# Output projection of a decoder layer: a float32 product per tile against a product of rounded halves

## The chip, the cores and the metric

The kernel runs on one core of a Trainium2 chip. The metric is the device time of one execution in microseconds (us). Nothing is computed on the host but the layout of the inputs.

## The reference

One decoder layer with normalisation after each part, over 2 sequences of 2048 tokens with 512 features: self-attention with 16 heads, cross-attention over 154 context tokens, a mixture of 64 experts with a shared expert. The change touches only the end of the first part:

```python
out = jnp.einsum('bhqk,bkhd->bqhd', attn, v).reshape(B, T, C)
return out @ Wo.T + bo
...
x = _layernorm(x + _L0_attn_ref(x, ...), axis=-1)   # (x - mean) / sqrt(var + 1e-5)
```

Everything is float32.

## The kernel before

`program` runs one stage after another: `self_attention`, `out_proj_norm`, `cross_attention`, `route_and_shared`, `experts`, `last_norm`. Each stage has its own semaphores and one instruction stream per engine, written out by hand: an engine does its instructions in the order of the code, and a wait holds everything behind it. There is no planner.

`out_proj_norm` (from L759) works on 32 tiles of 128 tokens. Self-attention has left its result transposed in HBM (`aT`). For each tile:

- SP loads the attention rows `at` (L797, 256 KB) and the residual `xr` (L799, 256 KB), two buffers each. Behind tile 2's it issues the loads that the next stage needs: weights, biases and two masks (L803, L805), some 2.6 MB in all. Behind the last tile's it loads the next stage's first rows.
- POOL adds the output bias to the residual, a tile ahead (L828).
- PE multiplies `at` by the output weights `wo` into one of two PSUM banks (L850): four float32 matmuls of 512 columns, which run as two passes each, so eight passes a tile. It does the product of tile t + 1 before it turns (transposes) the normalised rows of tile t (L856, four blocks).
- DVE adds product and residual (L876), takes mean and variance (L878, L881), inverts the deviation that ACT's square root gives (L895, L883) and normalises (L887).
- ACT stores the normalised rows (L897), copies the turned rows out of PSUM (L900) and stores them too (L902).

Ahead of the tiles, PE makes the cross-attention keys (L842) and DVE takes them out of PSUM (L870). `each_tile` writes tiles 0 to 2 and 29 to 31 out in straight code and runs the others in a rolled loop, two tiles a pass, in which waits compare with a register. `cross_attention` already does its own output projection as a product of halves (L1096, L1198, L1296) and its normalisation with Ln, Exp and a scaled copy on ACT (L1264, L1266, L1272).

Of the kernel before, what the change touches and what calls it, by code (L numbers as in the profile page):

```python
# [12 lines left out]
P = 128  # L13
# [689 lines left out]
        body(t, t % 2)  # L703


def before_end(t, ahead=0):
    return not isinstance(t, int) or t + ahead < NT

# [48 lines left out]


def out_proj_norm(nc, sems, early, cross, aT, x, bo, x1, x1T, mask, wqT, woT, bq, bk, bv, bo2):  # L759
    with ExitStack() as ctx:  # L760
        def sb(name, shape, dt=F32):
            return ctx.enter_context(nc.sbuf_tensor("on_" + name, shape, dt))
# [2 lines left out]
        passed = sem("passed")  # L765
        wo = early.o_weights; bob = sb("bob", [P, DM])
        identf, eps = cross.identf, cross.eps
        at = sb("at", [P, 2, KT, P]); xr = sb("xr", [P, 2, DM]); xb = sb("xb", [P, 2, DM])
        y = sb("y", [P, 2, DM]); stats = sb("stats", [P, 2, 6]); mv = sb("mv", [P, 2, 2])
        rstd = sb("rstd", [P, 2]); std = sb("std", [P, 2])  # L770
        xn = sb("xn", [P, 2, DM]); xnT = sb("xnT", [P, 2, KT, P])
        ops = [ctx.enter_context(nc.psum_tensor(f"on_o{i}", [P, DM], F32)) for i in range(2)]
        tps = [ctx.enter_context(nc.psum_tensor(f"on_t{i}", [P, DM], F32)) for i in range(2)]
        kps = [ctx.enter_context(nc.psum_tensor(f"on_k{i}", [P, 512], F32)) for i in range(NG)]
        w_in = sem("w_in"); k_done = sem("k_done"); ident_set = sem("ident_set"); a_in = [sem(f"a_in{i}") for i in range(2)]
        x_in = [sem(f"x_in{i}") for i in range(2)]
        o_done = sem("o_done"); xb_done = sem("xb_done"); y_done = sem("y_done"); nstep = sem("nstep"); mv_done = sem("mv_done"); std_done = sem("std_done"); rstd_done = sem("rstd_done")
        xn_done = sem("xn_done"); t_done = sem("t_done"); xnT_done = sem("xnT_done")
        xn_out = [sem(f"xn_out{i}") for i in range(2)]; xnT_out = [sem(f"xnT_out{i}") for i in range(2)]
        block = ctx.enter_context(nc.Block())  # L780
# [10 lines left out]
        @block.sync  # L791
        def _(sp):
            sp.dma_start(cross.bkb[:], bk).then_inc(w_in, 16)
            sp.dma_start(bob[:], bo.partition_broadcast(P)).then_inc(w_in, 16)
            def body(t, s):
                wait(sp, o_done, t - 1)
                sp.dma_start(at[:, s], aT.rearrange("k p t -> p k t")[:, :, bass.ds(t * P, P)]).then_inc(a_in[s], 16)  # L797
                wait(sp, xb_done, t - 1)
                sp.dma_start(xr[:, s], x[bass.ds(t * P, P), :]).then_inc(x_in[s], 16)  # L799
                if isinstance(t, int) and t == LEAD - 1:  # L800
                    for dst, src in ((cross.bvb[:], bv.partition_broadcast(P)), (cross.bqb[:], bq), (cross.wq[:], wqT),
                                     (cross.wo[:], woT), (cross.bob[:], bo2.partition_broadcast(P))):
                        sp.dma_start(dst, src).then_inc(cross.w_in, 16)  # L803
                    for n in range(2):
                        sp.dma_start(cross.mk[:, n], mask[n * P:(n + 1) * P, :]).then_inc(cross.mk_in[n], 16)  # L805
                if isinstance(t, int) and t == NT - 1:
                    for n in range(2):
                        sp.wait_ge(xnT_out[n], 16)
                        apart(sp, passed)
                        sp.dma_start(cross.xT[:, n], x1T[n]).then_inc(cross.xT_in[n], 16)  # L810
                        sp.wait_ge(xn_out[n], 16)
                        apart(sp, passed)
                        sp.dma_start(cross.xr[:, n], x1[n * P:(n + 1) * P, :]).then_inc(cross.x_in[n], 16)
            each_tile(sp, body)

        @block.gpsimd
        def _(pool):
# [19 lines left out]
        @block.tensor  # L837
        def _(pe):
            pe.wait_ge(early.first_in, 64)
            for g in range(NG):  # L840
                for k in range(KT):
                    mm = nc.tensor.matmul(kps[g][:, 0:BATCH * CTX], early.k_weights[:, k, g * P:(g + 1) * P],  # L842
                                          early.ctx[:, k].rearrange("p b c -> p (b c)"), start=k == 0, stop=k == KT - 1)
                mm.then_inc(k_done, 1)
            pe.wait_ge(ident_set, 3)
            def product(t, s):
                fetched(pe, a_in, t, s)
                wait(pe, y_done, t - 1)
                for k in range(KT):
                    mm = nc.tensor.matmul(ops[s][:], at[:, s, k], wo[:, k], start=k == 0, stop=k == KT - 1)  # L850
                mm.then_inc(o_done, 1)
            def turn(t, s):
                pe.wait_ge(xn_done, t + 1)
                wait(pe, xnT_done, t - 1)
                for k in range(KT):
                    mm = nc.tensor.transpose(tps[s][:, k * P:(k + 1) * P], xn[:, s, k * P:(k + 1) * P], identf[:])  # L856
                mm.then_inc(t_done, 1)
            product(0, 0)
            def body(t, s):
                if before_end(t, 1):  # L860
                    product(t + 1, 1 - s)
                turn(t, s)
            each_tile(pe, body)

        @block.vector
        def _(dve):
            dve.wait_ge(w_in, 32)
            for g in range(NG):
                dve.wait_ge(k_done, g + 1)
                dve.tensor_scalar(cross.keys[:, g].rearrange("p b c -> p (b c)"), kps[g][:, 0:BATCH * CTX],  # L870
                                  cross.bkb[:, g:g + 1], float(HD) ** -0.5, ALU.add, ALU.mult).then_inc(cross.set_up, 1)

            def body(t, s):
                dve.wait_ge(o_done, t + 1)
                dve.wait_ge(xb_done, t + 1)
                dve.tensor_tensor(y[:, s], ops[s][:], xb[:, s], ALU.add).then_inc(y_done, 1)  # L876
                dve.wait_ge(y_done, t + 1)
                dve.bn_stats(stats[:, s], y[:, s]).then_inc(nstep, 1)  # L878
                dve.wait_ge(nstep, t + 1)
                apart(dve, passed)  # L880
                dve.bn_aggr(mv[:, s], stats[:, s]).then_inc(mv_done, 1)  # L881
                dve.wait_ge(std_done, t + 1)
                dve.reciprocal(rstd[:, s:s + 1], std[:, s:s + 1]).then_inc(rstd_done, 1)  # L883
                dve.wait_ge(rstd_done, t + 1)
                stored(dve, xn_out, t, s)
                wait(dve, t_done, t - 1)
                dve.tensor_scalar(xn[:, s], y[:, s], mv[:, s, 0:1], rstd[:, s:s + 1], ALU.subtract, ALU.mult).then_inc(xn_done, 1)  # L887
            each_tile(dve, body)

        @block.scalar  # L890
        def _(act):
            act.wait_ge(ident_set, 3)
            def body(t, s):
                act.wait_ge(mv_done, t + 1)
                nc.scalar.activation(std[:, s:s + 1], mv[:, s, 1:2], ACT.Sqrt, bias=eps[:]).then_inc(std_done, 1)  # L895
                act.wait_ge(xn_done, t + 1)
                act.dma_start(x1[bass.ds(t * P, P), :], xn[:, s]).then_inc(xn_out[s], 16)  # L897
                act.wait_ge(t_done, t + 1)
                stored(act, xnT_out, t, s)
                nc.scalar.copy(xnT[:, s].rearrange("p k t -> p (k t)"), tps[s][:]).then_inc(xnT_done, 1)  # L900
                act.wait_ge(xnT_done, t + 1)
                act.dma_start(x1T[t], xnT[:, s]).then_inc(xnT_out[s], 16)  # L902
            each_tile(act, body)
            for s in range(2):
                act.wait_ge(xn_out[s], 16 * (NT // 2))
                act.wait_ge(xnT_out[s], 16 * (NT // 2))
# [1235 lines left out]
```

## Time and profile before

| | us |
|---|---|
| median of 3 runs | 3286.88 |
| lowest, highest | 3275.59, 3287.71 |
| the profiled execution | 3281.05 |
| its span, first to last instruction | 3279.3 |
| busy: PE, DVE, ACT, POOL | 2963.8, 2039.8, 1453.1, 1520.5 |
| mean granted TensorE clock | 0.961 of full speed |

The span is the profiler's own, from the first instruction to the last; the device time also holds what lies around it. Busy times are sums over the whole span, in which `out_proj_norm` is the stretch from about 1708 to 1862 us. The columns of each view are named at its first group of rows.

### The profile page before, as it was taken

Reading aid. Unit: us, or ns where it says so; the run is one execution under the profiler, and the core shown is the slowest. Engines: PE = TensorE matmul, PEld = TensorE weight load, DVE = VectorE, ACT = ScalarE, POOL = GpSimd, SP = SyncE. Lnnn points to the kernel's source line nnn. Section 1 sums busy time; section 2 is a strip of 40 time slices with the busy share of each in tenths; the row PEclk is TensorE's granted clock in tenths of the full one; section 3 lists DMA queues with packets and bytes.
Section 4 is the critical chain, followed back from the end, with each engine's and each line's share of the span. In section 5 each row is a group of like instructions: output and inputs, shape, how many; then the busy total and the mean of one; then the engine's idle time right before and its main releaser. Section 6 shows DMA issues by size and latency. Waiting matters only on the chain. (4 is left out here: it accounts for less than half of the span.)

```text
span 3279.3 us, 59175 instructions
## 1 busy us (share of the span) xinstructions
PE 2963.8 (90%) x19197; PEld 1934.0 (59%) x19197; DVE 2039.8 (62%) x4795; ACT 1453.1 (44%) x3375; POOL 1520.5 (46%) x1093
## 2 busy tenths in 40 slices
PE   7998999989989999898988979999799994999992
PEld 4444444444444444444434468888688883888882
DVE  4645646556465574554725568888477774777776
ACT  1443544434444444444442257777322222555551
POOL 3343443424434344243452234444377774665656
PEclk8999999999999999999999989999999996999996
DMA  4223022221221212212207522222222224999997
GB/s 114 62 64 82 7 74 79 58 63 32 75 78 44 66 44 74 78 31 67 66 30 253 189 84 88 79 82 84 84 71 68 68 61 140 258 254 259 257 254 265
DMA packets 185030, 343.33 MB, mean 105 GB/s; under 512 B 36136, under 2 KB 54696, under 8 KB 183848
## 3 DMA queue, kind: packets, MB, share of 16 engines
q1 hardware_dynamic: 135336, 250.90, 25.7%
q0 software_dynamic: 28800, 48.43, 6.8%
q10 hardware_dynamic: 20736, 41.95, 3.3%
q8 instruction: 92, 1.51, 0.2%
q14 instruction: 66, 0.54, 0.1%
HBM read 206.96 MB, written 83.89 MB: 89 GB/s over the span
## 5 line engine op out<-in xcount | busy, mean ns | idle before, releaser
L548 ACT ACTIVATE sa_probs<-sa_s 128x512 f32<-128x512 f32 (+3 forms) x1280 | 609.8, 540 | 692.9 <-PE sa_s L440 353.1
L334 POOL TENSOR_TENSOR sa_both<-sa_probs 128x2048 f32<-128x2048 f32 (+2 forms) x160 | 590.0, 3687 | 628.4 <-ACT sa_probs L548 616.9
L406 PE MATMUL sa_w<-sa_parts 96*128 96x512 f32 (+3 forms) x1280 | 515.0, 440 | 81.7 <-DVE sa_pmax L607 43.2
L440 PE MATMUL sa_s<-sa_parts 128*128 128x512 f32 (+3 forms) x1280 | 480.4, 409 | 27.3 <-ACT sa_probs L548 21.4
L607 DVE CUSTOM_DVE_ANT_0 sa_w<-sa_w,sa_maskS 128x512 f32<-128x512 f32 (+3 forms) x512 | 327.5, 649 | 238.7 <-PE sa_w L406 234.2
L406 PEld LDWEIGHTS sa_w<-sa_parts 96*128 96x128 f32 x1280 | 232.3, 195 | 409.4 <-issue 202.5
L611 DVE TENSOR_REDUCE sa_pmax<-sa_w 128x1 f32<-128x512 f32 (+3 forms) x768 | 422.7, 585 | 47.1 <-PE sa_w L406 44.0
L440 PEld LDWEIGHTS sa_s<-sa_parts 128*128 128x128 f32 x1280 | 242.0, 193 | 168.1 <-ACT sa_probs L548 96.6
L1519 POOL DMA_INDIRECT token_and_weight_of_slot<-rt_entry,rt_sl x256 | 261.0, 1020 | 124.4 <-issue 91.3
L458 PE MATMUL sa_pv<-sa_probs,sa_values 128*32 128x512 f32 (+3 forms) x2560 | 284.2, 538 | 0.0
L1252 ACT ACTIVATE xa_sm<-xa_sm,xa_nmax 128x154 f32<-128x154 f32 x512 | 209.4, 414 | 54.9 <-DVE xa_nmax L1175 54.9
L1831 POOL DMA_INDIRECT scratch_residual<-ex_y,ex_target x90 | 162.1, 1801 | 140.8 <-DMA scratch_residual<-ex_y,ex_target 109.2
L331 POOL COPY sa_both<-sa_probs 128x512 f32<-128x512 f32 x64 | 39.1, 611 | 342.7 <-ACT sa_probs L548 333.3
L1011 POOL TENSOR_TENSOR xa_pmain<-xa_sm,xa_rrec 128x2048 f32<-128x2048 f32 x32 | 115.9, 3622 | 109.8 <-DVE xa_rrec L1179 109.8
L469 PE MATMUL sa_pv<-sa_both,sa_ones 128*32 128x512 f32 (+1 forms) x1280 | 155.0, 556 | 0.0
L1893 PE MATMUL ex_yps<-ex_w2h,ex_hTh 128*128 128x512 f32 x540 | 148.1, 412 | 4.6 <-ACT ex_hTh L1926 4.3
L1876 PE MATMUL ex_h<-ex_xeT,ex_w1h 128*128 128x256 f32 x1080 | 145.4, 284 | 2.4 <-ACT ex_w1h L1905 2.4
L1041 PE MATMUL xa_qps<-cross_xT,cross_wq 128*128 128x128 f32 x1024 | 128.9, 281 | 20.4 <-DMA cross_xT<-scratch_x_T 16.2
L1876 PE MATMUL ex_h<-ex_xeT,ex_w3h 128*128 128x256 f32 x1080 | 145.3, 283 | 0.0
L1876 PEld LDWEIGHTS ex_h<-ex_xeT,ex_w1h 128*128 128x128 f32 x1080 | 139.7, 190 | 6.7 <-issue 2.8
L1876 PEld LDWEIGHTS ex_h<-ex_xeT,ex_w3h 128*128 128x128 f32 x1080 | 136.8, 190 | 0.0
L1041 PEld LDWEIGHTS xa_qps<-cross_xT,cross_wq 128*128 128x128 f32 x1024 | 123.1, 197 | 21.3 <-issue 21.3
(236 smaller groups left out, 5360.0 us busy)
## 6 DMA issues: line engine op xcount, KB each, us to landing
list_w<-in_w SPq DMA_DIRECT2D x138, 512.0 KB, 5.6
sa_parts<-early_halves SPq DMA_DIRECT2D x384, 128.0 KB, 2.4
early_xt<-in_xT SPq DMA_DIRECT2D x32, 1024.0 KB, 5.7
scratch_attention_T<-sa_oT SPq DMA_DIRECT2D x32, 256.0 KB, 2.4
on_at<-scratch_attention_T SPq DMA_DIRECT2D x32, 256.0 KB, 3.1
on_xr<-in_x SPq DMA_DIRECT2D x32, 256.0 KB, 3.4
scratch_x<-on_xn ACTq DMA_DIRECT2D x32, 256.0 KB, 2.1
scratch_x_T<-on_xnT ACTq DMA_DIRECT2D x32, 256.0 KB, 3.4
```

The costliest lines, as they stand in the source:

```text
L334: pool.tensor_tensor(both[:, p % 2, :, 0:w], probs[:, even, :, 0:w], probs[:, odd, :, 0:w], ALU.add).then_inc(both_ready, 1)
L406: nc.tensor.matmul(ps[:, 0:w], qparts[0:3 * HD, h, q0:q0 + P], kparts[0:3 * HD, h, k0:k0 + w], start=True, stop=True).then_inc(work_ready, 1)
L440: mm = nc.tensor.matmul(ps[:, 0:w], kparts[:, h, kb * P:(kb + 1) * P], qparts[:, h, q0:q0 + w], start=True, stop=not diag)
L458: mm = nc.tensor.matmul(pvbank[0][a:a + HD, 0:w], values[:, kb, h, :], probs[:, r % NPB, h, 0:w], start=kb == NKB - 1, stop=kb == QB * chu ...
L548: nc.scalar.activation(probs[:, r % NPB, h, 0:w], sbank[n % NSB][:, 0:w], ACT.Exp).then_inc(exp_done, 1)
L607: dve.tensor_tensor_reduce(out=wbank[b][:, 0:width_], in0=wbank[b][:, 0:width_], in1=maskS[:, 0:width_], scale=1.0, scalar=LOWEST, op0=ALU ...
L611: dve.tensor_reduce(pmax[:, j * GH + h, s:s + 1], wbank[b][:, 0:width_], AX.X, ALU.max).then_inc(work_free[b], 1)
L1041: mm = nc.tensor.matmul(qps[:, g * P:(g + 1) * P], wq[:, k, g * P:(g + 1) * P], xT[:, s, k], start=k == 0, stop=k == KT - 1)
L1252: nc.scalar.activation(sm[:, s, h], sm[:, s, h], ACT.Exp, bias=nmax[:, s, h:h + 1], accum_out=rsum[:, s, h:h + 1]).then_inc(exp_done, 1)
L1519: pool.indirect_dma_start(out=table, out_offset=bass.IndirectOffsetOnAxis(ap=sl[:, s, k:k + 1], axis=0), in_=entry[:, s, k], in_offset=Non ...
L1831: pool.indirect_dma_start(out=res, out_offset=bass.IndirectOffsetOnAxis(ap=target[:, s, j:j + 1], axis=0), in_=y[:, s, j], in_offset=None, ...
L1876: mm = nc.tensor.matmul(bank[f][:, 0:UNIT], wt[:, s, a, k, f * P:(f + 1) * P], xeT[:, s, b, k], start=k == 0 and n == 0, stop=k == KT - 1 ...
```

## The change

Only `out_proj_norm` changes, with a new loop helper. The attention rows and the weights are each split into a rounded part (float32r, index 0, made by ACT) and what is left of it (index 1, the difference made by DVE). The product becomes the sum of three terms, high by high, high by low and low by high: twelve matmul passes instead of eight. The rows are loaded two tiles ahead into four buffers; the halves have two. PE runs the product two tiles ahead of the turn. ACT computes the inverse deviation as Exp(-0.5 Ln(var + eps)) and normalises by a scaled copy; DVE makes the shift that this copy needs. Each engine's order within a tile is new, and the rolled loop takes four tiles a pass: tiles 0 to 3 and 28 to 31 are straight code.

```diff
+def each_tile_of_four(eng, body):
+    for t in range(4):
+        body(t, t)
+    with eng.Fori(0, (NT - 8) // 4) as i:
+        for s in range(4):
+            body(eng.snap(i * 4 + (4 + s)), s)
+    for t in range(NT - 4, NT):
+        body(t, t % 4)
...
+    TERMS = ((0, 0), (0, 1), (1, 0))
...
-        at = sb("at", [P, 2, KT, P]); xr = sb("xr", [P, 2, DM]); xb = sb("xb", [P, 2, DM])
+        at = sb("at", [P, 4, KT, P]); ath = sb("ath", [P, 2, 2, KT, P], F32R); woh = sb("woh", [P, 2, KT, DM], F32R); xr = sb("xr", [P, 2, DM]); xb = sb("xb", [P, 2, DM])
...
-        rstd = sb("rstd", [P, 2]); std = sb("std", [P, 2])
+        rstd = sb("rstd", [P, 2]); logv = sb("logv", [P, 2]); shift = sb("shift", [P, 2])
...
-        w_in = sem("w_in"); k_done = sem("k_done"); ident_set = sem("ident_set"); a_in = [sem(f"a_in{i}") for i in range(2)]
+        w_in = sem("w_in"); k_done = sem("k_done"); ident_set = sem("ident_set"); a_in = [sem(f"a_in{i}") for i in range(4)]
...
         def _(sp):
             sp.dma_start(cross.bkb[:], bk).then_inc(w_in, 16)
             sp.dma_start(bob[:], bo.partition_broadcast(P)).then_inc(w_in, 16)
-            def body(t, s):
-                wait(sp, o_done, t - 1)
-                sp.dma_start(at[:, s], aT.rearrange("k p t -> p k t")[:, :, bass.ds(t * P, P)]).then_inc(a_in[s], 16)
+            def load_attention(t, s4):
+                wait(sp, a_low, t - 3)
+                sp.dma_start(at[:, s4], aT.rearrange("k p t -> p k t")[:, :, bass.ds(t * P, P)]).then_inc(a_in[s4], 16)
+            for t in range(2):
+                load_attention(t, t)
+            def body(t, s4):
+                s = s4 % 2
+                if before_end(t, 2):
+                    load_attention(t + 2, (s4 + 2) % 4)
                 wait(sp, xb_done, t - 1)
                 sp.dma_start(xr[:, s], x[bass.ds(t * P, P), :]).then_inc(x_in[s], 16)
                 if isinstance(t, int) and t == LEAD - 1:
...
                         sp.wait_ge(xn_out[n], 16)
                         apart(sp, passed)
                         sp.dma_start(cross.xr[:, n], x1[n * P:(n + 1) * P, :]).then_inc(cross.x_in[n], 16)
-            each_tile(sp, body)
+            each_tile_of_four(sp, body)
         @block.gpsimd
         def _(pool):
...
                                           early.ctx[:, k].rearrange("p b c -> p (b c)"), start=k == 0, stop=k == KT - 1)
                 mm.then_inc(k_done, 1)
             pe.wait_ge(ident_set, 3)
-            def product(t, s):
-                fetched(pe, a_in, t, s)
+            def product(t, s4):
+                s = s4 % 2
+                pe.wait_ge(a_high, t + 1)
+                pe.wait_ge(a_low, t + 1)
                 wait(pe, y_done, t - 1)
-                for k in range(KT):
-                    mm = nc.tensor.matmul(ops[s][:], at[:, s, k], wo[:, k], start=k == 0, stop=k == KT - 1)
+                for n, (a, b) in enumerate(TERMS):
+                    for k in range(KT):
+                        mm = nc.tensor.matmul(ops[s][:], ath[:, s, a, k], woh[:, b, k], start=k == 0 and n == 0,
+                                              stop=k == KT - 1 and n == len(TERMS) - 1)
                 mm.then_inc(o_done, 1)
             def turn(t, s):
                 pe.wait_ge(xn_done, t + 1)
...
                 for k in range(KT):
                     mm = nc.tensor.transpose(tps[s][:, k * P:(k + 1) * P], xn[:, s, k * P:(k + 1) * P], identf[:])
                 mm.then_inc(t_done, 1)
+            pe.wait_ge(wo_high, 1)
+            pe.wait_ge(wo_low, 1)
             product(0, 0)
-            def body(t, s):
-                if before_end(t, 1):
-                    product(t + 1, 1 - s)
-                turn(t, s)
-            each_tile(pe, body)
+            product(1, 1)
+            def body(t, s4):
+                if before_end(t, 2):
+                    product(t + 2, (s4 + 2) % 4)
+                turn(t, s4 % 2)
+            each_tile_of_four(pe, body)
         @block.vector
         def _(dve):
+            dve.wait_ge(wo_high, 1)
+            dve.tensor_tensor(woh[:, 1], wo[:], woh[:, 0], ALU.subtract).then_inc(wo_low, 1)
             dve.wait_ge(w_in, 32)
             for g in range(NG):
                 dve.wait_ge(k_done, g + 1)
                 dve.tensor_scalar(cross.keys[:, g].rearrange("p b c -> p (b c)"), kps[g][:, 0:BATCH * CTX],
                                   cross.bkb[:, g:g + 1], float(HD) ** -0.5, ALU.add, ALU.mult).then_inc(cross.set_up, 1)
-            def body(t, s):
+            def measure(t, s):
                 dve.wait_ge(o_done, t + 1)
                 dve.wait_ge(xb_done, t + 1)
+                wait(dve, xn_done, t - 1)
                 dve.tensor_tensor(y[:, s], ops[s][:], xb[:, s], ALU.add).then_inc(y_done, 1)
                 dve.wait_ge(y_done, t + 1)
                 dve.bn_stats(stats[:, s], y[:, s]).then_inc(nstep, 1)
                 dve.wait_ge(nstep, t + 1)
                 apart(dve, passed)
                 dve.bn_aggr(mv[:, s], stats[:, s]).then_inc(mv_done, 1)
-                dve.wait_ge(std_done, t + 1)
-                dve.reciprocal(rstd[:, s:s + 1], std[:, s:s + 1]).then_inc(rstd_done, 1)
+            def shifts(t, s):
                 dve.wait_ge(rstd_done, t + 1)
-                stored(dve, xn_out, t, s)
-                wait(dve, t_done, t - 1)
-                dve.tensor_scalar(xn[:, s], y[:, s], mv[:, s, 0:1], rstd[:, s:s + 1], ALU.subtract, ALU.mult).then_inc(xn_done, 1)
-            each_tile(dve, body)
+                dve.wait_ge(mv_done, t + 1)
+                dve.tensor_scalar(shift[:, s:s + 1], mv[:, s, 0:1], rstd[:, s:s + 1], -1.0, ALU.mult, ALU.mult).then_inc(shift_done, 1)
+            def low_half(t, s4):
+                dve.wait_ge(a_high, t + 1)
+                dve.tensor_tensor(ath[:, s4 % 2, 1], at[:, s4], ath[:, s4 % 2, 0], ALU.subtract).then_inc(a_low, 1)
+            for t in range(2):
+                low_half(t, t)
+            def body(t, s4):
+                s = s4 % 2
+                if before_end(t, 2):
+                    low_half(t + 2, (s4 + 2) % 4)
+                measure(t, s)
+                if not isinstance(t, int) or t > 0:
+                    shifts(t - 1, 1 - s)
+            each_tile_of_four(dve, body)
+            shifts(NT - 1, (NT - 1) % 2)
         @block.scalar
         def _(act):
             act.wait_ge(ident_set, 3)
-            def body(t, s):
+            def deviation(t, s):
                 act.wait_ge(mv_done, t + 1)
-                nc.scalar.activation(std[:, s:s + 1], mv[:, s, 1:2], ACT.Sqrt, bias=eps[:]).then_inc(std_done, 1)
+                nc.scalar.activation(logv[:, s:s + 1], mv[:, s, 1:2], ACT.Ln, bias=eps[:]).then_inc(log_done, 1)
+                act.wait_ge(log_done, t + 1)
+                wait(act, shift_done, t - 1)
+                nc.scalar.activation(rstd[:, s:s + 1], logv[:, s:s + 1], ACT.Exp, scale=-0.5).then_inc(rstd_done, 1)
+            def norm(t, s):
+                act.wait_ge(shift_done, t + 1)
+                stored(act, xn_out, t, s)
+                wait(act, t_done, t - 1)
+                nc.scalar.activation(xn[:, s], y[:, s], ACT.Identity, bias=shift[:, s:s + 1], scale=rstd[:, s:s + 1]).then_inc(xn_done, 1)
                 act.wait_ge(xn_done, t + 1)
                 act.dma_start(x1[bass.ds(t * P, P), :], xn[:, s]).then_inc(xn_out[s], 16)
+            def store_turned(t, s):
                 act.wait_ge(t_done, t + 1)
                 stored(act, xnT_out, t, s)
                 nc.scalar.copy(xnT[:, s].rearrange("p k t -> p (k t)"), tps[s][:]).then_inc(xnT_done, 1)
                 act.wait_ge(xnT_done, t + 1)
                 act.dma_start(x1T[t], xnT[:, s]).then_inc(xnT_out[s], 16)
-            each_tile(act, body)
+            nc.scalar.preload_act_table_set("natural_log_exp_and_others")
+            act.wait_ge(early.first_in, 64)
+            nc.scalar.copy(woh[:, 0], wo[:]).then_inc(wo_high, 1)
+            def high_half(t, s4):
+                act.wait_ge(a_in[s4], ((t - s4) // 4) * 16 + 16)
+                wait(act, o_done, t - 1)
+                nc.scalar.copy(ath[:, s4 % 2, 0], at[:, s4]).then_inc(a_high, 1)
+            for t in range(2):
+                high_half(t, t)
+            def body(t, s4):
+                s = s4 % 2
+                if before_end(t, 2):
+                    high_half(t + 2, (s4 + 2) % 4)
+                deviation(t, s)
+                if not isinstance(t, int) or t > 0:
+                    norm(t - 1, 1 - s)
+                    store_turned(t - 1, 1 - s)
+            each_tile_of_four(act, body)
+            norm(NT - 1, (NT - 1) % 2)
+            store_turned(NT - 1, (NT - 1) % 2)
             for s in range(2):
                 act.wait_ge(xn_out[s], 16 * (NT // 2))
                 act.wait_ge(xnT_out[s], 16 * (NT // 2))
```

## Rows read from the trace of the kernel before

**Rows 1.** Windows, steady part of the stage: length, busy by engine, granted clock, DMA, GB/s

```profile
1770.00:1790.00 20.00, 20.00 (x63) 9.84 (x62) 11.99 (x27) 4.96 (x11) 6.92 (x6) 1.00 0.79 269
```

**Rows 2.** Waits in the stage: engine line <- releaser: total us, times, longest

```profile
DVE on_y L876 <- PE on_o L850: 34.4, 31, 9.3
```

**Rows 3.** Timeline, two steady tiles: start, length (us), engine, line, operation

```profile
1784.92 0.69 DVE L876 TENSOR_TENSOR on_y<-on_o,on_xb 128x512 f32<-128x512 f32 x1 [0.78 <-PE on_o L850]
...
1786.90 0.29 ACT L895 ACTIVATE on_std<-on_mv,cross_eps 128x1 f32<-128x1 f32 x1 [0.85 <-DVE on_mv L881]
...
1788.59 0.60 PE L856 MATMUL on_t<-cross_identf,on_xn 128*128 128x128 f32 x4
1788.80 0.69 DVE L876 TENSOR_TENSOR on_y<-on_o,on_xb 128x512 f32<-128x512 f32 x1 [0.59 <-PE on_o L850]
...
1789.03 3.60 PE L850 MATMUL on_o<-early_xt,on_at 128*128 128x512 f32 x8
...
1789.35 0.59 ACT L900 COPY on_xnT<-on_t 128x512 f32<-128x512 f32 x1 [2.16 <-PE on_t L856]
...
1790.10 0.34 ACTq L902 DMA_DIRECT2D scratch_x_T<-on_xnT  x1
...
1790.59 0.29 ACT L895 ACTIVATE on_std<-on_mv,cross_eps 128x1 f32<-128x1 f32 x1 [0.65 <-DVE on_mv L881]
...
1791.35 0.55 DVE L887 TENSOR_SCALAR on_xn<-on_y,on_mv,on_rstd 128x512 f32<-128x512 f32 x1 [0.27 <-DVE on_rstd L883]
...
1792.04 0.14 PEld L856 LDWEIGHTS on_t<-cross_identf,on_xn 128*128 128x128 f32 x1 [0.24 <-DVE on_xn L887]
```

**Rows 4.** Timeline, the product that starts after the stall

```profile
1739.08 6.37 PE L850 MATMUL on_o<-early_xt,on_at 128*128 128x512 f32 x8 [6.51 <-DMA on_at<-scratch_attention_T]
```

**Rows 5.** Windows, the stall: the columns of rows 1

```profile
1732.00:1736.00 4.00, 0.57 (x5) 0.34 (x3) 2.08 (x5) 0.88 (x2) 0.00 (x0) 1.00 1.02 401
1736.00:1740.00 4.00, 0.92 (x1) 0.50 (x2) 0.20 (x1) 0.00 (x0) 0.19 (x1) 0.71 1.09 378
```

**Rows 6.** Timeline, the start of the stage

```profile
1718.99 0.45 PEld L850 LDWEIGHTS on_o<-early_xt,on_at 128*128 128x128 f32 x2
...
1719.45 0.54 DVE L870 TENSOR_SCALAR cross_keys<-on_k,cross_bkb 128x308 f32<-128x308 f32 x1 [1.54 <-PE on_k L842]
```

**Rows 7.** Timeline, the last tile of the stage

```profile
1857.80 0.66 PE L856 MATMUL on_t<-cross_identf,on_xn 128*128 128x128 f32 x4 [2.52 <-DVE on_xn L887]
1858.49 0.59 ACT L900 COPY on_xnT<-on_t 128x512 f32<-128x512 f32 x1 [1.53 <-PE on_t L856]
1859.11 0.34 ACTq L902 DMA_DIRECT2D scratch_x_T<-on_xnT  x1
```

**Rows 8.** Timeline, cross attention: its product of halves and its normalisation

```profile
2058.70 0.29 ACT L1264 ACTIVATE xa_logv<-xa_mv,cross_eps 128x1 f32<-128x1 f32 x1
...
2058.87 3.01 PE L1096 MATMUL xa_ops<-xa_woh,xa_oTh 128*128 128x512 f32 x12
2059.02 0.20 ACT L1266 ACTIVATE xa_rstd<-xa_logv 128x1 f32<-128x1 f32 x1
...
2059.68 0.82 ACT L1272 ACTIVATE xa_xn<-xa_y,xa_shift,xa_rstd 128x512 f32<-128x512 f32 x1 [0.45 <-DVE xa_shift L1194]
...
2060.68 0.34 ACTq L1276 DMA_DIRECT2D scratch_x<-xa_xn  x1
2061.11 0.59 ACT L1296 CAST xa_oTh<-xa_pvps 128x512 fp32r<-128x512 f32 x1 [0.62 <-ACT xa_xn L1272]
```

**Rows 9.** Groups by shape, casts and differences: count, busy, mean ns, idle before

```profile
L1905 ACT CAST ex_w3h<-list_w 128x1024 fp32r<-128x1024 f32 x46 | 48.1, 1045 | 0.0
...
L1926 ACT CAST ex_hTh<-ex_hT 128x256 fp32r<-128x256 f32 x90 | 36.3, 403 | 38.1 <-DVE ex_hT L1975 38.1
```

**Rows 10.** Timeline, the split of the weights in cross attention

```profile
1863.78 1.90 ACT L1304 CAST xa_woh<-cross_wo 128x2048 fp32r<-128x2048 f32 x1
1865.78 2.29 DVE L1234 TENSOR_TENSOR xa_woh<-cross_wo,xa_woh 128x2048 fp32r<-128x2048 f32 x1 [8.04 <-ACT xa_woh L1304]
```

More of the change, by code:

```diff
@@ L774, in out_proj_norm @@
         kps = [ctx.enter_context(nc.psum_tensor(f"on_k{i}", [P, 512], F32)) for i in range(NG)]
-        w_in = sem("w_in"); k_done = sem("k_done"); ident_set = sem("ident_set"); a_in = [sem(f"a_in{i}") for i in range(2)]
+        w_in = sem("w_in"); k_done = sem("k_done"); ident_set = sem("ident_set"); a_in = [sem(f"a_in{i}") for i in range(4)]
         x_in = [sem(f"x_in{i}") for i in range(2)]
-        o_done = sem("o_done"); xb_done = sem("xb_done"); y_done = sem("y_done"); nstep = sem("nstep"); mv_done = sem("mv_done"); std_done = sem("std_done"); rstd_done = sem("rstd_done")
+        o_done = sem("o_done"); xb_done = sem("xb_done"); y_done = sem("y_done"); nstep = sem("nstep"); mv_done = sem("mv_done"); a_high = sem("a_high"); a_low = sem("a_low"); wo_high = sem("wo_high"); wo_low = sem("wo_low"); log_done = sem("log_done"); rstd_done = sem("rstd_done"); shift_done = sem("shift_done")
         xn_done = sem("xn_done"); t_done = sem("t_done"); xnT_done = sem("xnT_done")
```

## The prediction

> **What bounds the kernel now.** I read the page first, then the windows, the waits and the timeline of the stage that the change touches. The page's own chain of waits only reaches back over the last normalisation of the kernel, so it says nothing here. The windows show the stage's steady part to be TensorE's: busy 20.00 us of 20 at a granted clock of 1.00, DVE 12 us, ACT 5 us, DMA share 0.79 [rows 1]. The waits agree: the longest in the stage that is not some idle engine's own is DVE's for the product, 34.4 us [rows 2]. The timeline gives the period: the add of L876 starts at 1784.92 and again at 1788.80, 3.88 us a tile, of which eight passes of the product are 3.60 us [rows 3]. One stretch is not TensorE's. The cross-attention weights are loaded behind tile 2's rows, DMA is full, and the product that should have started at about 1732.6 starts at 1739.08 after 6.51 us of waiting [rows 4]; while it waits, the granted clock stays 1.00 in one window and falls to a mean of 0.71 in the next [rows 5], so that the product takes 6.37 instead of 3.60 us. The stall costs about 6.5 + 2.8 = 9.3 us. The first product starts at 1718.99 [rows 6], the last store is issued at 1859.11 [rows 7].
>
> **The change, part by part.** *Product.* Twelve passes on rounded halves replace eight. The trace has such a product in cross attention: twelve in 3.01 us [rows 8], against 3.60 [rows 3]. TensorE gains 0.6 us a tile; with the turn (0.60, or about 0.43 where the next pass overlaps it) its own work is about 3.4 us.
>
> *What the halves cost.* ACT gets a cast of 512 columns a tile: between 403 ns (256) and 1045 (1024) [rows 9], by a straight line 0.62 us. DVE gets a difference of 512, as wide as the add of 0.69 us [rows 3]. DVE loses the normalising operation (0.55) [rows 3] and the reciprocal; ACT gets it at 0.82 us, and Ln with Exp, 0.52 us from the start of one to the end of the other [rows 8], for Sqrt (0.29).
>
> *Order.* This is what decides, so I wrote each engine's new order down. Within one tile step ACT does: cast(t+2), Ln and Exp(t), normalise(t-1), copy and store of the turned rows (t-1). DVE: difference(t+2), add, statistics and aggregate(t), shift(t-1). PE: product(t+2), turn(t). An engine takes its instructions in order, so a wait at the head holds all behind it. Follow one ring: turn(t-2) frees ACT's copy(t-2); behind it on ACT stands cast(t+2); DVE's difference(t+2) waits for that cast, and behind the difference on DVE stands the add of tile t, though its product is long done; Ln(t) waits for the aggregate(t); behind Ln and Exp(t) on ACT stands normalise(t-1); turn(t-1) waits for that. From turn(t-2) to turn(t-1) is one tile, and nothing on the way overlaps anything else on the way. The second buffers do not open the ring, because it closes by order and not by a buffer. Product(t+1) runs beside it, between the two turns.
>
> The length of the ring has two versions, for the tiles in straight code (the hops as in rows 7) and those in the rolled loop (as in rows 3). Turn's start to the copy: 0.69 [rows 7], 0.76 [rows 3]. Copy's start to its store's issue: 0.62, 0.75. Issue 0.34 and 0.09 until ACT's next instruction (2060.68 + 0.34 to 2061.11) [rows 8]: 0.43. Cast 0.62. Hop to DVE: 0.03 (1858.46 to 1858.49), 0.14 (end of the normalising operation 1791.90 to 1792.04). Difference 0.69 and 0.03 of gap. Add to the deviation's start: 1.79 for one tile, 1.98 for the other [rows 3], taken as 1.79 and as the mean, 1.88. Ln and Exp 0.52. Normalise 0.05 + 0.82. Hop to PE 0.03, 0.14. Sums: 6.33 and 6.83 us; with 1.98 it is 6.93. The ring is thus nearly twice TensorE's present 3.88, and the gain of the product is idle time.
>
> *The start.* The weights' cast (1.90) and difference (2.29) [rows 10] lie beside the key products, which end at about 1719.4; the cover has several us to spare. But DVE takes the differences of tiles 0 and 1 only behind its fourth key operation, which ends at 1719.45 + 0.54 = 1719.99 [rows 6]. So product(0) starts at about 1720.8 instead of 1719.0, ends at 1723.8; cast(2) 0.62 and difference(2) 0.69 with a hop, then add(0) at 1725.2, Ln(0) at 1727.1, Exp ends at 1727.6; cast(3) and difference(3) to 1729.0, Ln(1) at 1730.9, Exp ends 1731.4, normalise(0), turn(0) at 1732.3.
>
> *The sum.* Turns 1 to 3 are straight code: 3 x 6.33 = 19.0. Tiles 4 to 27 are rolled: 24 x 6.83 = 163.9. Turn 28: 6.3. From tile 30 there is no cast ahead: add(30) waits only for normalise(28), and turns 29 and 30 follow at 0.05 + 1.88 + 0.52 + 0.87 and a hop, 3.4 us each; turn 31 after copy, issue and normalise, 2.7 us. So turn(31) starts at 1931.0, and its store is issued 1.31 later [rows 7]: 1932.3, against 1859.11. That is 73 us longer. All tiles at 6.33 make it 61 us, all at 6.93 make it 76.
>
> *Loads.* Tiles 0 to 4 are now fetched before the cross-attention weights. SP waits for a difference two tiles back, long done. The rows of tile 5 and the residual of tile 3 are issued behind the weights at about 1727; in the present run everything issued there had landed by 1740 [rows 5], and tile 3's add is due only at about 1742. So the stall of 9.3 us goes, but into the ring, which is late next; the 73 us are counted from ends and contain it already. POOL's add is done a tile ahead. A megabyte a tile at 6.8 us asks for half the DMA share of now. The store's two issues on ACT: the one of the turned rows is in the ring, the other lies beside the turn. The table load of the present Sqrt goes, and may go once more at the start of cross attention; neither stands on a path that ends a stage.
>
> The profiled run took 3281.05 us (span 3279.3), 5.8 below the median of the runs, 3286.88. 3281 + 73 = 3354.
>
> **Rivals.** *A, the ring with a slow clock.* TensorE would work some 3.4 us and then rest some 3.4 us in each tile. In the stall the clock was still 1.00 in the first window of the rest and fell in the second [rows 5]; a shorter rest that comes back in every tile is in no row of mine. At the lower level a product took 6.37 for 3.60 [rows 4], a factor of 1.77. Twelve passes would take 5.3 and the turn 1.2 us, still under the ring; only the turn's 0.5 us lies in the ring, 28 x 0.5 = 14 us more: 3368. For it: the rest comes in every tile. Against: at the lower level TensorE would work 6.5 of 7.3 us, which is not what stood before the fall in rows 5.
> The Trainium skill (page TensorE: Matmul & The Clock Gate, section "HAM oscillation — how this bites in real kernels") says that a loop in which the array has to wait in every pass is put back to the slow clock in every pass. By that rule rival A holds and the time is 3368; by the row alone, with the clock held, it is 3354.
>
> *B, on the other side: the steps overlap after all.* If the ring spanned two tiles (a wait that I place at the head of a queue being met earlier than I think), the bound would be the fullest engine. That is ACT: cast 0.62, Ln and Exp 0.52, normalise 0.87, copy 0.59, two issues at 0.43 and up to 0.3 of hops, 3.4 to 3.8 us, against 3.88 now. Over 28 tiles that gives 2 to 13 us, and the stall's 9.3 less 2 at the start: 3281 - 17 = 3264. It decides from the point at which the ring falls under 3.9 us. For it: every engine's own work is below that, and no engine but ACT comes near. Against: each link of the ring is written as a wait or as an order.
>
> *C, half of it:* a link or two, such as the store's issue, don't stand in series: 5.3 to 6.2 us a tile, by the same sum 3313 to 3339. *D, the product doesn't gain:* if the twelve took 3.6 or more, the time would not change, as TensorE rests; it would show in the product's row alone.
>
> **How the numbers follow.** Forecast 0.73 (own range 3341 to 3364), A 0.13, C 0.07, B 0.07. About 0.5%, 16 us, is what a measurement of this kernel can tell from no change. Only B is below that bound: faster 0.06, same 0.02, slower 0.92. The range from 3332 to 3376 holds the forecast, most of A and the upper end of C.
>
> **What would show it.** Right: in the windows of the stage TensorE busy about half, all engines with idle time, and about 6.8 us from add to add; the waits headed by the turn for the normalised rows, by the difference for the cast, and by the copy for the turn; the add of tile t starting right behind difference(t+2), with its product done one tile before; the DMA share near 0.45 and no stall at 1732; turns of the last three tiles at 3.4 and 2.7 us. Wrong: a period below 5.5 us, or an add that starts when its product ends, would mean that the ring is not closed; a period above 7.2 with a clock near 0.5 would mean A.

## The result, and the profile after

| | us |
|---|---|
| median after (4 runs) | 3345.45 (3343.63 to 3348.20) |
| median before, same chip (4 runs) | 3284.93 (3275.59 to 3287.71) |
| ratio after to before | 1.0191, 95% interval 1.0169 to 1.0212 |
| profiled execution after | 3346.18, span 3344.4, mean clock 0.953 |

The change makes the kernel 60 us slower. Between the two profiled executions it is 65.1 us, in the span as in the whole time, and nearly all of it lies in the one stage: from the first product to the issue of the last store are now 206.9 us (1719.07 to 1926.00), against 140.1 [rows 6, 7].

Three windows of the stage after, with the columns of [rows 1]:

```profile
1730.00:1750.00 20.00, 12.18 (x51) 9.36 (x52) 7.00 (x15) 7.33 (x15) 5.36 (x4) 0.90 0.78 248
...
1770.00:1790.00 20.00, 12.21 (x50) 8.97 (x49) 6.99 (x15) 7.58 (x16) 3.81 (x3) 0.91 0.49 161
...
1810.00:1830.00 20.00, 12.91 (x47) 9.73 (x46) 6.99 (x15) 6.84 (x16) 3.80 (x3) 0.78 0.48 158
```

PE was busy 20.00 of 20 us; now, over the nine windows from 1730 to 1910, it is busy 11.38 to 14.29 us, and DVE, ACT and POOL less than half. In the steady windows DMA moves some 160 GB/s where it moved 269. A stage in which nothing is full is waiting for itself, and the waits from 1719 to 1920 say where (the columns of [rows 2]):

```profile
POOL on_xb L849 <- DVE on_y L907: 145.5, 27, 7.4
DVE on_ath L921 <- ACT on_ath L968: 118.4, 30, 4.4
ACT on_logv L941 <- DVE on_mv L912: 73.4, 31, 2.4
PE on_t L881 <- ACT on_xn L950: 67.8, 29, 3.6
...
ACT on_xnT L957 <- PE on_t L881: 27.6, 30, 1.3
...
DVE on_y L907 <- PE on_o L874: 1.5, 1, 1.5
```

Read from the bottom: DVE's wait for the product, 34.4 us before [rows 2], is gone. The four lines above it hand on to each other: the difference waits for the cast, the logarithm for the statistics, the turn for the normalised rows, the copy for the turn. POOL, at the head, waits for the add, and nothing waits for POOL: no line of the view names it behind the arrow. The timeline of one tile, from turn to turn, shows them in their order:

```profile
1776.96 4.48 PE L874 MATMUL on_o<-on_woh,on_ath 128*128 128x512 f32 x12
...
1782.68 0.65 PE L881 MATMUL on_t<-cross_identf,on_xn 128*128 128x128 f32 x4 [1.24 <-ACT on_xn L950]
...
1783.09 3.03 PE L874 MATMUL on_o<-on_woh,on_ath 128*128 128x512 f32 x12
1783.37 0.59 ACT L957 COPY on_xnT<-on_t 128x512 f32<-128x512 f32 x1 [0.82 <-PE on_t L881]
1784.11 0.34 ACTq L959 DMA_DIRECT2D scratch_x_T<-on_xnT  x1
1784.69 0.62 ACT L968 CAST on_ath<-on_at 128x512 fp32r<-128x512 f32 x1 [0.74 <-ACT on_xnT L957]
1785.34 0.69 DVE L921 TENSOR_TENSOR on_ath<-on_at,on_ath 128x512 fp32r<-128x512 f32 x1 [4.01 <-ACT on_ath L968]
1785.95 0.68 DVE L907 TENSOR_TENSOR on_y<-on_o,on_xb 128x512 f32<-128x512 f32 x1
...
1787.74 0.29 ACT L941 ACTIVATE on_logv<-on_mv,cross_eps 128x1 f32<-128x1 f32 x1 [2.43 <-DVE on_mv L912]
1788.06 0.20 ACT L944 ACTIVATE on_rstd<-on_logv 128x1 f32<-128x1 f32 x1
...
1788.17 0.80 ACT L950 ACTIVATE on_xn<-on_y,on_shift,on_rstd 128x512 f32<-128x512 f32 x1
...
1789.10 0.65 PE L881 MATMUL on_t<-cross_identf,on_xn 128*128 128x128 f32 x4 [2.99 <-ACT on_xn L950]
1789.51 4.60 PE L874 MATMUL on_o<-on_woh,on_ath 128*128 128x512 f32 x12
```

From the first turn on, every line but the products follows on the one above it, with at most 0.24 us between them (the statistics between add and logarithm are left out here). The product (3.03 us, 3.60 before in [rows 3]) lies beside them. The add of L907 has no wait of its own: it starts as the difference ends. Its product is the first line, which was over at 1781.44, 4.5 us earlier. That product and the one in the last line, 4.48 and 4.60 us, ran in part at the lower clock: from 1789.50 to 1794.20 the granted clock is 0.64.

The stage's two ends:

```profile
1719.07 8.44 PE L874 MATMUL on_o<-on_woh,on_ath 128*128 128x512 f32 x36 [1.32 <-DVE on_ath L921]
...
1729.95 0.66 PE L881 MATMUL on_t<-cross_identf,on_xn 128*128 128x128 f32 x4 [2.44 <-ACT on_xn L950]
...
1924.23 1.12 PE L881 MATMUL on_t<-cross_identf,on_xn 128*128 128x128 f32 x4 [1.98 <-ACT on_xn L950]
...
1926.00 0.34 ACTq L959 DMA_DIRECT2D scratch_x_T<-on_xnT  x1
```

The stall of [rows 4] is gone, as three products' worth of rows stand ready; nobody can tell from the time, since the ring was later anyway.

### The profile page after: what moved, and what is told of

Read it like the earlier page. It is cut to its first block and busy times, and to the rows that moved or that the text cites. A ratio compares the mean times of both kernels' runs of the same rounds, so it can differ in the third digit from the quotient of the medians.

```text
span 3344.4 us, 59553 instructions
## 1 busy us (share of the span) xinstructions
PE 2972.4 (89%) x19325; PEld 1975.1 (59%) x19325; DVE 2042.4 (61%) x4796; ACT 1505.8 (45%) x3472; POOL 1520.3 (45%) x1093
```

## The experiments

"Stage" is the time from the first product to the start of the last copy of turned rows: 139 to 140 us before, 206 after. The kernel before, timed beside them, had medians of 3280.0 to 3282.6; after was not timed again beside them, so that differences from its 3345.45 carry some 2 to 5 us of scatter, and the stage, read from the traces, is the closer measure.

| run | median, us | ratio to before, 95% | stage, us |
|---|---|---|---|
| after | 3345.45 | 1.0191, 1.0169 to 1.0212 | 206.3 |
| e1_add_first | 3276.71 | 0.9993, 0.9982 to 1.0004 | 133.9 |
| e4_issue_late | 3320.28 | 1.0132, 1.0115 to 1.0148 | 180.1 |
| e2_product_twice | 3350.88 | 1.0224, 1.0206 to 1.0241 | 210.4 |
| e3_one_term | 3353.40 | 1.0234, 1.0217 to 1.0251 | 213.9 |
| e5_order | 3303.66 | 1.0060, 1.0045 to 1.0076 | 165.7 |
| e7_both | 3264.21 | 0.9942, 0.9926 to 0.9957 | 123.6 |
| e9_no_ring_weights | 3291.39 | 1.0031, 1.0019 to 1.0042 | 149.8 |
| e6_loads_ahead | 3281.45, one run | | 135.8 |
| e10_both_weights_later | 3257.55 | 0.9926, 0.9913 to 0.9938 | 116.8 |
| e11_before_weights_later | 3283.17 | 1.0005, 0.9994 to 1.0015 | 142.8 |

**The ring opened on DVE.** Only the order of DVE's instructions changes:

```diff
-                if before_end(t, 2):
-                    low_half(t + 2, (s4 + 2) % 4)
                 measure(t, s)
                 if not isinstance(t, int) or t > 0:
                     shifts(t - 1, 1 - s)
+                if before_end(t, 2):
+                    low_half(t + 2, (s4 + 2) % 4)
```

> DVE does the add, the statistics and the shift of a tile ahead of the difference two tiles on; nothing else is changed. Ring by order: the difference, the add and the statistics leave the ring, and what is left from turn to turn is copy, issue, cast, Ln, Exp and normalise, about 0.7 + 0.75 + 0.43 + 0.62 + 0.05 + 0.5 + 0.05 + 0.8 + 0.14 = 4.1 us a tile for 6.6 now: 3345 - 28 x 2.5 = 3275 (3268 to 3285), and the add starts while ACT copies. Added work (each engine simply has more to do in a tile, whatever the order): every instruction is still there, 3345. Slow clock: TensorE rests less, but its clock alone was worth 0.5 us in every second tile: not below 3335.

It took 3276.71 us: all of the loss is gone, with the same instructions on every engine, and the stage is 72.4 us shorter than in after. The timeline of this run, from turn to turn:

```profile
1782.21 0.65 PE L881 MATMUL on_t<-cross_identf,on_xn 128*128 128x128 f32 x4 [0.18 <-ACT on_xn L950]
1782.21 0.69 DVE L907 TENSOR_TENSOR on_y<-on_o,on_xb 128x512 f32<-128x512 f32 x1 [0.63 <-ACT on_xn L950]
...
1784.22 0.62 ACT L968 CAST on_ath<-on_at 128x512 fp32r<-128x512 f32 x1 [0.74 <-ACT on_xnT L957]
1784.75 0.29 ACT L941 ACTIVATE on_logv<-on_mv,cross_eps 128x1 f32<-128x1 f32 x1
...
1786.11 0.65 PE L881 MATMUL on_t<-cross_identf,on_xn 128*128 128x128 f32 x4 [0.51 <-ACT on_xn L950]
```

The add now starts with the turn, not 3.3 us behind it, and the statistics are ready when ACT has done its cast, so that the logarithm waits for nothing. The period is 3.90 us; what is left of the ring is turn, copy, issue, cast, Ln, Exp and normalise.

**The ring shortened on ACT.** The store of the turned rows is issued one step later, behind the next cast:

```diff
...
                 if before_end(t, 2):
                     high_half(t + 2, (s4 + 2) % 4)
+                if not isinstance(t, int) or t > 1:
+                    issue_turned(t - 2, s)
                 deviation(t, s)
...
```

> ACT issues the store of the turned rows behind the next cast in place of ahead of it, in the time in which it waits for the statistics; nothing else is changed. Ring by order: only the wait for the copy and the issue leave the ring, 0.43 to 0.73 us from the copy's end to the cast's start less about 0.1, so 0.3 to 0.6 a tile: 3345 - 28 x 0.5 = 3331 (3326 to 3338). Added work or a slow clock: ACT is busy 7.5 us of 20, its issue lies in idle time either way, 3345.

It took 3320.28, 25 us less than after (26.2 in the stage), and about 11 less than expected. Copy, cast and issue in this run:

```profile
1781.90 0.59 ACT L957 COPY on_xnT<-on_t 128x512 f32<-128x512 f32 x1 [0.82 <-PE on_t L881]
1782.38 0.62 ACT L970 CAST on_ath<-on_at 128x512 fp32r<-128x512 f32 x1
1782.65 0.34 ACTq L961 DMA_DIRECT2D scratch_x_T<-on_xnT  x1
```

In after the cast started 0.73 us behind the end of the copy; here it starts 0.11 before it. An issue between these two ACT instructions costs not its 0.34 us but 0.84 here: the wait for the copy's result, the issue, the start of the next, and the overlap that copy and cast have in a row. Over the 28 such gaps the mean is 0.71 us in after and -0.10 in this run, 0.80 a tile and 22.5 us in all, most of what was measured. The prediction's link had the wait and the issue, but not that overlap.

**Is the product on the path?** Two kernels change the arithmetic's size alone, to 24 passes and to 4:

```diff
-    TERMS = ((0, 0), (0, 1), (1, 0))
+    TERMS = ((0, 0), (0, 1), (1, 0)) * 2
```

> The three terms of the product are summed twice, 24 passes a tile (the projected rows are doubled, nothing else is changed). Ring by order: 24 passes are some 5.6 us between two turns and still end before the next turn is due, so nothing gets longer; TensorE hardly rests, its clock holds, all turns take 0.66 in place of 1.1 in every second tile, and the period falls from a mean of 6.6 to 6.4: 3345 - 7 = 3338 (3332 to 3346), granted clock of the stage 1.0. Product on the path (the twelve passes are part of what a tile takes): 32 x 2.6 = 83 us more, 3428.

```diff
-    TERMS = ((0, 0), (0, 1), (1, 0))
+    TERMS = ((0, 0),)
```

> Only the high by high term of the product is left, 4 passes a tile (the two low terms are left out; both halves are still made). Ring by order: no gain from a third of the product; TensorE rests longer, more turns run at the lower clock, the period goes to 6.6 to 6.9: 3345 to 3354. Product on the path: 32 x 8 x 0.216 = 55 us less, 3290.

Twice the product adds 5 us, a third of it takes nothing off: away from the stage's ends it is not on the path. Twice the product missed its expectation in sign. One window of each (columns of [rows 1]), 24 passes first, then 4:

```profile
1790.00:1810.00 20.00, 18.71 (x86) 14.54 (x85) 6.99 (x15) 7.75 (x16) 3.88 (x3) 1.00 0.49 160
```

```profile
1790.00:1810.00 20.00, 8.46 (x24) 5.73 (x24) 6.12 (x15) 7.41 (x15) 3.62 (x3) 0.51 0.48 157
```

With 24 passes PE is nearly always busy, the clock stays at 1.00 (2.4 GHz), every turn but the last takes 0.60 to 0.66 us, and turns 1 to 28 take 180.9 us against after's 185.1: a gain of 4.2 where I expected 7. So the slow clock is not what makes after slow, either. What I left out are the ends, where PE's queue is the path: turn(0) stands behind three products of 5.5 us and comes 16.5 us after the first product instead of 10.9; the turn of tile 29 comes 6.0 after its forerunner instead of 3.2; and the stage started 2 us later. -4.2 + 5.6 + 2.8 + 2.1 is 6.3, of which the profiled executions show 5.3. With 4 passes the granted clock is 0.51 in this window (0.50 to 0.74 in those from 1730 to 1850), every turn takes 1.11 or 1.12 us, as after's turns at the lower level (1.2 GHz) do, and the mean period is 6.9.

**A better order that is none.** On top of the first experiment, ACT does Ln and Exp, the normalise, then the cast, and the copy last:

```diff
-                if before_end(t, 2):
-                    high_half(t + 2, (s4 + 2) % 4)
                 deviation(t, s)
                 if not isinstance(t, int) or t > 0:
                     norm(t - 1, 1 - s)
+                if before_end(t, 2):
+                    high_half(t + 2, (s4 + 2) % 4)
+                if not isinstance(t, int) or t > 0:
                     store_turned(t - 1, 1 - s)
```

> As the run with the add ahead of the difference, and ACT also makes the cast of the tile two on behind the normalise of the tile before, so that the cast leaves the ring and lies beside the turn. Ring by order: ACT's own chain is left, Ln and Exp 0.5, normalise and its issue 1.3, cast 0.6, copy and its issue 1.3, about 3.7 us a tile for 3.9: 3277 - 28 x 0.2 = 3271 (3262 to 3278). The loads of the cross-attention weights hold the residual of tile 3 as before. If what is left after the first cut is not ACT's order but TensorE or DMA: 3277.

It took 3303.66, 33 more than expected: a miss. The waits from 1770 to 1830 name it:

```profile
DVE on_ath L921 <- ACT on_ath L968: 30.8, 12, 2.8
ACT on_logv L941 <- DVE on_mv L912: 23.5, 12, 2.0
```

As in after, only POOL's wait for the add stands ahead of these two in the list. With the cast behind the normalise there is a second ring: add(t), statistics, Ln and Exp(t), normalise(t-1), cast(t+2), difference(t+2) on DVE, and behind that on DVE the add(t+1). One tile again, 5.3 us (turns at 1782.41 and 1787.74). I had moved an instruction out of one ring and had not drawn the other. The same mistake stands in the next kernel, which has four buffers for `y` so that an add need not wait for an earlier normalise, issues the turned rows' store between Ln and Exp, and loads the next stage's two weights later. Its core:

```diff
...
+                deviation(t, s, s4)
+                if not isinstance(t, int) or t > 0:
+                    norm(t - 1, 1 - s, (s4 + 3) % 4)
                 if before_end(t, 2):
                     high_half(t + 2, (s4 + 2) % 4)
-                deviation(t, s)
                 if not isinstance(t, int) or t > 0:
-                    norm(t - 1, 1 - s)
-                    store_turned(t - 1, 1 - s)
+                    store(t - 1, 1 - s)
+                    copy_turned(t - 1, 1 - s)
...
```

> An attempt at a faster version: the add ahead of the difference, four buffers for the sum of product and residual, ACT's order Ln, issue of the turned rows two back, Exp, normalise, cast, issue, copy; and the two large cross-attention weights are loaded behind tile 3 and tile 28 and not both behind tile 2. Ring by order: no ring shorter than TensorE's own work is left, 3.1 to 3.3 us a tile, DMA share about 0.95, and tile 3's residual no longer waits (5 us): 3277 - 28 x 0.65 - 5 = 3254 (3246 to 3262). If DMA cannot give a megabyte in 3.3 us beside the work, 3.5 to 3.9 us a tile: 3262 to 3272.

It took 3291.39, 37 more than expected. The same two links, from add to add:

```profile
1783.71 0.68 DVE L910 TENSOR_TENSOR on_y<-on_o,on_xb 128x512 f32<-128x512 f32 x1
...
1787.01 0.60 ACT L977 CAST on_ath<-on_at 128x512 fp32r<-128x512 f32 x1
...
1787.64 0.69 DVE L924 TENSOR_TENSOR on_ath<-on_at,on_ath 128x512 fp32r<-128x512 f32 x1 [2.04 <-ACT on_ath L977]
...
1788.25 0.68 DVE L910 TENSOR_TENSOR on_y<-on_o,on_xb 128x512 f32<-128x512 f32 x1
```

4.5 us, and no buffer in it: the fourth `y` could not help.

**Both edits together**, the first experiment's and the late issue:

> The two cuts tried one by one, together: the add ahead of the difference, and the turned rows' store issued behind the next cast. Ring by order: the period falls from 3.9 us by the 0.8 that the late issue was worth alone, until DVE's add waiting for the normalise two tiles back and TensorE's own 3.1 to 3.4 us hold it: 3.3 to 3.4 us, 3277 - 28 x 0.5 = 3263 (3256 to 3270). If the two cuts were worth the same thing (the second hides what the first removed): 3277.

It took 3264.21, within 1.2 us. Turns come every 3.35 us (1781.32, 1784.67, 1788.04), and the window reads

```profile
1770.00:1790.00 20.00, 19.93 (x96) 15.05 (x95) 17.88 (x31) 14.10 (x30) 7.93 (x7) 1.00 0.96 314
```

PE is full again, now at 3.4 us a tile instead of 3.88: with the ring cut in both places the gain of the product shows. One stall is left, at tile 3, where the residual's rows stand behind the next stage's weights:

```profile
1738.88 0.69 DVE L907 TENSOR_TENSOR on_y<-on_o,on_xb 128x512 f32<-128x512 f32 x1 [7.92 <-POOL on_xb L849]
```

**That stall.** Two kernels ask for it on the side of before. The first gives before the attention rows two tiles ahead, in four buffers, with the loop of four tiles that they need, and nothing else:

```diff
...
+                if before_end(t, 2):
+                    load_attention(t + 2, (s4 + 2) % 4)
...
```

> The kernel before with one part of the change alone: attention rows loaded two tiles ahead into four buffers. The product of tile 3 no longer waits at 1732 to 1739, but its add still needs the residual that is loaded behind the weights and lands at about 1740: the stage's stall shrinks from 9 to about 5 us, the period stays 3.87, 3277 by one look. If the rows alone made the stall, it goes wholly, 3272.

The product of tile 3 no longer waits, but its add does: the same line reads 1742.52 with 4.95 us for POOL, whose residual is late. The stage is 3.4 us shorter; one run can't resolve that. The second leaves before's loads in place and issues `wo` of the next stage behind tile 29 instead of tile 2:

```diff
...
+                if isinstance(t, int) and t in (LEAD - 1, NT - 3):
+                    dst, src = (cross.wq[:], wqT) if t == LEAD - 1 else (cross.wo[:], woT)
+                    sp.dma_start(dst, src).then_inc(cross.w_in, 16)
```

> The kernel before with only this: the second large cross-attention weight is loaded behind tile 29 and not behind tile 2. It shows what the loads alone are worth: half of the bytes ahead of tile 3's rows, so the stall of 9.3 us falls to some 4: 3282 - 5 = 3277 (3272 to 3281). If the stall has another cause than these bytes: 3282.

No gain, 1.0005: a miss. The products behind the two loads:

```profile
1739.80 3.70 PE L853 MATMUL on_o<-early_xt,on_at 128*128 128x512 f32 x8 [3.64 <-DMA on_at<-scratch_attention_T]
...
1851.67 6.55 PE L853 MATMUL on_o<-early_xt,on_at 128*128 128x512 f32 x8 [4.88 <-DMA on_at<-scratch_attention_T]
```

The first stall is 3.64 instead of 6.51 [rows 4] and keeps its clock; the second is new. With rows one tile ahead each load in the line stalls by itself.

**The best of it.** Both edits, with `wq` issued behind tile 3 and `wo` behind tile 28:

> The two cuts together, and the two large cross-attention weights loaded behind tile 3 and behind tile 28 and not both behind tile 2. With the two cuts the add of tile 3 waited 7.9 us for a residual behind these loads, and the clock fell after it. Ring by order, stall now open: the wait goes or falls to 1 to 2 us, 3264 - 8 = 3256 (3251 to 3261). If the wait only moves to the tile behind the one weight that is left there: 3264.

3257.55 us, 0.74% less than before and 88 less than after. The stretch of the stall is now

```profile
1730.00:1750.00 20.00, 18.76 (x92) 14.40 (x91) 14.39 (x29) 13.16 (x29) 7.89 (x6) 1.00 0.99 340
```

with PE at work and the clock held, as the rows stand two tiles ahead.

## Why the prediction was right, step by step

The time was 3345.45, in the forecast's own range of 3341 to 3364 and 8.6 below its 3354.

*The ring.* It is there, link by link, in the order that the prediction wrote down. Its two cuts are what shows it: without one instruction more or less, the order on DVE alone makes the stage 72 us shorter, the issue's place on ACT alone 26. Rival B (steps that overlap) and the bound by an engine fall with that, and with 4 and 24 passes, which move the time by 5 to 8 us, not by the 55 less or 83 more of a product on the path. C falls too: the mean period of 6.61 us lies above its 6.2, and the issue that it took out of the series stands in it.

*Its length* was the term that was off. Predicted 6.83 us a rolled tile; four turns at the full clock in a row (1789.10 to 1815.15) take 6.29, 6.95, 6.39 and 6.42, in the mean 6.51. The links of the tile from 1782.68:

| link | predicted | measured |
|---|---|---|
| turn to copy | 0.76 | 0.69 |
| copy to issue | 0.75 | 0.74 |
| issue to cast | 0.43 | 0.58 |
| cast to difference | 0.76 | 0.65 |
| difference to add | 0.72 | 0.61 |
| add to Ln | 1.88 | 1.79 |
| Ln to normalise | 0.57 | 0.43 |
| normalise to turn | 0.96 | 0.93 |
| sum | 6.83 | 6.42 |

I took a gap between instructions in a row on one engine where two of them overlap by 0.08 us, and the mean of two values for add to deviation where the lower holds. Against that, every fourth tile is longer by some 0.6 (6.95 of the four above): where the rolled loop comes round, ACT's cast starts 0.56 us behind the end of the issue instead of 0.09 to 0.24 (1784.11 + 0.34 to 1784.69), and the rest lies in the gaps around Exp and the normalise. I did not have that link; that the loop's own turn-round makes it is argued from its place, not shown by a run.

*The sum.* The last store was to be issued at 1932.3 and was at 1926.00. Of the 6.3 us, 2.35 are the start: the first product at 1719.07 instead of 1720.8, and 10.9 instead of 11.5 us from there to turn(0). The first of these lies within scatter: the first products of the kernels here start anywhere from 1719.1 to 1723.0. 4.1 are turns 1 to 28, 185.1 us instead of 189.2: the rolled ones were shorter by 4.4 in all, the straight ones longer by 0.3. The last three turns came in 9.15 instead of 9.5, with 3.23, 3.28 and 2.64 us for the predicted 3.4, 3.4 and 2.7; and the last turn was slow by 0.46. The stages behind gave back another 1.8 us, and the four runs' medians, not the profiled ones, differ by 60.5 instead of 65.1. In the sum itself the straight links add up to 6.32, not 6.33, and the 76 us given for all tiles at 6.93 hold for the rolled ones alone (all 28 make it 78).

*Luck.* Two terms that the sum did not hold made up for part of what its links had too much: the slow turns, 4.1 us, and the loop's come-round, about 6 x 0.55 = 3.3 us. By this estimate the median would else have been near 3338, below the forecast's own range. The mechanism does not hang on that; the fit of the number does.

*Rival A* was true in part. Turns of 1.11 or 1.12 us appear, eight of the 28, with two in between (0.85, 0.98): 8 x 0.45 + 0.2 + 0.3 = 4.1 us of the 14 that it priced. The clock fell and came back from tile to tile, with a window's mean of 0.78 to 0.91. The Trainium skill (page TensorE: Matmul & The Clock Gate, section "HAM oscillation — how this bites in real kernels") tells its rule, by which the clock falls again in every pass, of a loop whose wait is long enough, a condition that the prediction left out. The turns of the kernel with 4 passes, all slow, agree with it; those of this one, eight slow of 28, do not.

*Product, start, loads, D:* twelve passes took 3.03 us (3.01 predicted). The split of the weights stayed hidden: its difference was over at 1712.81, and the 1.32 us of wait ahead of the first product are for the first tile's difference. The stall went into the ring. That the loads had landed by 1740 is not to be read from [rows 5], which hold no landing; in the trace before, POOL's wait for the residual ended at 1739.81. POOL's longest wait for the residual is 12.1 us and no add waits for it. The gain of the product was worth nothing as long as the ring was whole.

*What would show it:* PE is busy 57 to 71% rather than half, since its passes at the lower clock count longer; the DMA share is 0.45 to 0.50 from 1750 on, as predicted. The mean period is 6.61, not 6.8.

## What to carry to other kernels

When a change spreads a tile's work over more engines, write each engine's order down and follow, from any instruction, what it waits for or stands behind, until you come back to it one tile on: the longest such way is the period, however idle the engines, unless one engine's own work in a tile is longer still. A further buffer that is no link of that way does not help, as the fourth `y` did not here. Then do the same for the order that you want to put in its place: two of the orders here cut one ring and closed another. And an operation that is cheap by its duration (a DMA issue on ACT) is to be priced by the link that it adds between its neighbours, 0.8 us for 0.34.

## What the runs showed of the hardware

*DVE beside POOL.* In the kernel with both edits the difference, 0.69 us in after, takes 0.68 to 1.81. It is long where POOL's bias add runs at the time:

```profile
1782.66 1.29 POOL L849 TENSOR_TENSOR on_xb<-on_xr,on_bob 128x512 f32<-128x512 f32 x1 [1.61 <-DMA on_xr<-in_x]
...
1783.31 1.18 DVE L921 TENSOR_TENSOR on_ath<-on_at,on_ath 128x512 fp32r<-128x512 f32 x1
...
1786.40 1.30 POOL L849 TENSOR_TENSOR on_xb<-on_xr,on_bob 128x512 f32<-128x512 f32 x1 [2.45 <-DMA on_xr<-in_x]
...
1786.82 1.42 DVE L921 TENSOR_TENSOR on_ath<-on_at,on_ath 128x512 fp32r<-128x512 f32 x1
```

POOL ends at 1783.95 and 1787.70, the difference at 1784.49 and 1788.24: 0.54 us behind it both times, whenever it began. The statistics, which read one tile, keep their 0.69 beside POOL. The Trainium skill (page SBUF — State Buffer, section "SBUF: two separate sides") says that a DVE operation with two inputs in SBUF and one of POOL lock each other out for the length of an instruction; these rows agree, in that the difference ends only behind POOL's add, though the 0.54 us that is left then is less than the 0.69 it takes alone. The other way round shows once in this run: a difference from 1766.41 to 1767.09 and POOL's add from 1766.58, which takes 1.66 us instead of 1.29. No run here takes it apart. At 3.35 us a tile PE is full (19.93 of 20) and DVE is not, but DVE's 17.88 busy us are partly this wait.

*The clock.* In after it went to and fro between 1.2 and 2.4 GHz from tile to tile for the whole stage, with turns of 0.66 and 1.11 us beside each other. With 4 passes every turn took 1.11 or 1.12 us; with 24 the windows show 1.00. The kernel of the better order that is none has a PE that rests in every tile as well, and its windows from 1750 to 1850 show 1.00 all the same. Why the one order holds the clock and the other does not, no run here shows.
